# A graph layer and a mixture of experts on one core: gating and first-choice routing in batches beside the update, and an expert layer without its transposes

## The reference

```python
h = layernorm(x)
msg = silu(concat(h[ei], h[ej], d2) @ mW1 + mb1)
msg = silu(layer_norm(msg) @ mW2 + mb2)
agg = segment_sum(msg, ei)
x = x + h + silu(concat(h, agg) @ uW1 + ub1) @ uW2 + ub2
t = layernorm(x)                       # tokens of the experts
probs = softmax(t @ router_w.T)
rw, re = top_k(probs, 2); rw = rw / rw.sum(-1)
out = t
for e in range(8):
    y = gelu(t @ w1[e] + b1[e]) @ w2[e] + b2[e]
    out = out + combine[:, e] * y      # rw where e is one of the node's two, else 0
return x + out
```

## Time and profile before

| | |
|---|---|
| three runs, median (lowest to highest) | 2658.04 us (2655.57 to 2659.8) |
| the profiled execution | 2656.25 us, of which the span is 2654.4 us |
| PE / PEld busy | 2380.0 (90%) / 2044.3 (77%) |
| DVE / ACT / POOL busy | 2007.8 (76%) / 1716.5 (65%) / 1353.1 (51%) |
| TensorE's granted clock, mean | 0.949 of full |
| DMA | 265.16 MB, mean 100 GB/s |

### The profile page before, as it was taken

The page is one execution under the profiler, slowest core; times in us unless marked ns, Lnnn a source line. Parts: engine busy times, 40 slices in busy tenths (PEclk is TensorE's granted clock), DMA queues, the critical chain, the costliest instruction groups (busy, mean ns, idle before and its releaser), DMA issues. The chain is left out here.

```text
span 2654.4 us, 61287 instructions
## 1 busy us (share of the span) xinstructions
PE 2380.0 (90%) x15214; PEld 2044.3 (77%) x15215; DVE 2007.8 (76%) x6154; ACT 1716.5 (65%) x5986; POOL 1353.1 (51%) x1342
## 2 busy tenths in 40 slices
PE   4399999789999999999999999999999889119997
PEld 4288887568888888888888888888888779117886
DVE  8999999477777777777777777777777656546653
ACT  1777777567777777777777777777777556233432
POOL 2067777465555555555555555555555101267666
PEclk7599999989999999999999999999999989559998
DMA  7011111243232323232322332323235299156675
GB/s 151 1 34 29 34 34 29 86 114 91 87 92 87 91 87 91 87 91 87 91 87 89 89 91 87 91 87 91 87 91 86 62 289 307 67 204 203 208 123 65
DMA packets 155377, 265.16 MB, mean 100 GB/s; under 512 B 31249, under 2 KB 99440, under 8 KB 154917
## 3 DMA queue, kind: packets, MB, share of 16 engines
q0 software_dynamic: 64656, 147.39, 21.2%
q1 hardware_dynamic: 90623, 116.59, 14.6%
HBM read 190.85 MB, written 73.02 MB: 99 GB/s over the span
## 5 line engine op out<-in xcount | busy, mean ns | idle before, releaser
L1056 POOL DMA_INDIRECT work<-dst_half,stage_i x848 | 811.6, 957 | 758.3 <-PE ps L1264 582.5
L1247 PE MATMUL ps<-W2c,work 128*128 128x256 f32 x3392 | 802.3, 379 | 0.0
L1247 PEld LDWEIGHTS ps<-W2c,work 128*128 128x128 f32 x3392 | 612.0, 190 | 70.7
L1082 DVE TENSOR_TENSOR agg<-agg,ps 125x256 f32 x848 | 354.2, 418 | 254.0 <-PE ps L1264 246.3
L1188 ACT ACTIVATE work<-ps 128x512 f32<-128x512 f32 x424 | 251.9, 594 | 351.5 <-PE ps L1264 351.4
L1264 PE MATMUL ps<-work 128*125 128x256 f32 x1696 | 435.2, 379 | 1.3 <-ACT work L1209 1.3
L1203 ACT ACTIVATE work<-work 128x256 f32<-128x256 f32 x848 | 341.4, 404 | 53.6 <-DVE work L1109 50.1
L1161 DVE SCALAR_TENSOR_TENSOR work<-ps,work,b2c 128x256 f32<-128x256 f32 x848 | 368.4, 476 | 0.0
L1238 PE MATMUL ps<-ablk,work 128*128 x2544 | 351.1, 275 | 16.3 <-DVE work L1130 10.4
L519 POOL DMA_INDIRECT edge_records<-stage,work x208 | 262.6, 1263 | 176.2 <-PE ps L946 113.2
L1195 ACT ACTIVATE work<-work 128x256 f32<-128x256 f32 x848 | 340.8, 406 | 0.3
(11 more groups left out here) (280 smaller groups left out, 3366.8 us busy)
## 6 DMA issues: line engine op xcount, KB each, us to landing
work<-tile_sources SPq DMA_DIRECT2D x106, 250.0 KB
first_choice_tokens<-work SPq DMA_DIRECT2D x14, 1028.0 KB
work<-dst_half,stage_i POOLq DMA_INDIRECT x848, 2.8
second_choice_tokens<-work SPq DMA_DIRECT2D x14, 516.0 KB
work<-first_choice_tokens SPq DMA_DIRECT2D x28, 258.0 KB, 3.7
work<-second_choice_tokens SPq DMA_DIRECT2D x28, 258.0 KB, 2.9
work<-first_choice_tokens SPq DMA_DIRECT2D x28, 256.0 KB, 3.4
update_node_half<-work SPq DMA_DIRECT2D x25, 250.0 KB, 2.2
```

The source lines that it names most:

```text
L1056: pool.indirect_dma_start(bg[:, r, u, :], None, dstd, bass.IndirectOffsetOnAxis(ap=stage_i[:, c:c + 1], axis=0)).then_inc(gath[r], 16)
L1082: v.tensor_tensor(d, d, ps[0:NB, (7, 0)[a.mod(2)], u * D:(u + 1) * D], ALU.add).then_inc(agg_add, 1)
L1247: last = t_.matmul(ps[:, 5 + s, u * D:(u + 1) * D], sT[:, a.mod(RT), u, k], W2c[:, k], start=(k == 0), stop=(k == KC - 1))
```

## The change

It has three parts.

1. **Gating and routing in batches.** The 25 pairs of the update are split in batches of 9, 9 and 7 pairs. As soon as the logits of a batch exist, its gating chain runs in the four steps that follow, on the DVE behind that step's update work (`shift_logits`, `choose`, `count`, `place`). The pipeline has 36 steps instead of 31. The tiles of the first batch are routed two in a step (steps 19 to 27), those of the second three in a step (28 to 33), and the 14 of the last all in step 35. A table now can't be sorted by expert as a whole: each batch opens new tiles where its expert's last one is full, and `state` carries this from batch to batch. The table of experts is sent to memory and read back beside the last 14 tiles.
2. **Pads.** The harmless rows are kept in a table `pad_rows` in memory, which SP fills in the preparation, from `rec`. They are copied from there to the two tables in the message stage, two DMAs more in each of its 106 loads of one-hot rows, and three tiles of each table at the end of the preparation. The 28 stores of the update, and the wait for the tile they were made from, are gone. The waits for `zeros_out` now include the four stores to `pad_rows`.
3. **Experts.** The first matrix is multiplied with its weights as the stationary operand (eight products of 128 x 128 by 128 in place of four of 128 x 128 by 256 for a pair), so the result comes out transposed and L1988 and ACT's copy L1932 go. The bias is now one value for a partition, and ACT adds it with the Gelu (four of 128 x 128 for a pair). [...] The first bias on the DVE goes. The lags are shorter, and `y_ps` has four banks.

```diff
+BATCHES = (9, 9, 7)
+PACE = (2, 3, BK)
...
 # preparation, SP
+                empty = rec[:, :, :].rearrange("p g f -> p (g f)")[:, 0:2 * XB]
+                for h in range(XD // 2):
+                    sp.dma_start(padd[2 * h * P:2 * (h + 1) * P, :].rearrange("(p d) w -> p (d w)", p=P),
+                                 empty).then_inc(zeros_out, 16)
...
+                sp.wait_ge(pad_rows_out, 16)
+                for g in range(TAILS // 2, XC):
+                    d = g % XD * P
+                    for k in range(K2):
+                        sp.dma_start(xsd[k][g * P:(g + 1) * P, :], padd[d:d + P, 0:(XW if k else XB)]).then_inc(xpads_out, 16)
...
 # preparation, DVE
-                dve.wait_ge(zeros_out, 64)
+                dve.wait_ge(zeros_out, 64 + 8 * XD)
                 block_one_hots(NG - 1)
...
 # messages, SP, in each load of one-hot rows
+                        d = m.mod(2 * XD) * (P // 2)
+                        slots = bass.ds(m.of(P // 2), P // 2)
+                        for k in range(K2):
+                            sp.dma_start(xsd[k][slots, :], padd[d:d + P // 2, 0:(XW if k else XB)]).then_inc(xpads_out, 16)
...
 # update
+        def routed(m):
+
+            n = 0
+            for b, t0, t1, first in batches:
+                n = max(n, min(n + PACE[b] * max(m - first - 4, 0), t1))
+            return BK if m >= USTEPS else n
...
 # update, DVE (choose, count and place are the old chain cut to a batch, place with 5 wide and some 15 small operations)
+                for m in range(USTEPS):
+                    step(Step(0, 1, m))
+                    for b, t0, t1, first in batches:
+                        if m == first:
+                            shift_logits(b, t0, t1)
+                        if m == first + 1:
+                            choose(b, t0, t1)
+                        if m == first + 2:
+                            count(b, t0, t1)
+                        if m == first + 3:
+                            place(b, t0, t1)
+                    for t in range(routed(m), routed(m + 1)):
+                        r = t % RS0
+                        dve.wait_ge(slots_ready, batch_of(t) + 1)
+                        wait(dve, first_out[r], 16 * (t // RS0))
+                        v.tensor_scalar(ts0[n_, r, 0:D], agg[n_, t, :], mv3[n_, t:t + 1, 1], mv3[n_, t:t + 1, 0], ALU.mult, ALU.add)
+                        v.tensor_copy(ts0[n_, r, D:XW], idgate[n_, 0, t, :]).then_inc(row_ready, 1)
...
 # experts
-        LXT, L1, LG1, L2H, LHT, L2 = 1, 2, 3, 4, 5, 6
+        LXT, L1, LG1, L2 = 1, 2, 3, 4
...
 # experts, DVE, at the head of step m
+                    a = m - LXT
+                    if 0 <= a < XP:
+                        wait(dve, h_ps, a - RW + 1)
+                        for u in range(2):
+                            o = offs[2 * (b + L2 - LXT) + u]
+                            v.tensor_copy(w1p[:, a % RW, u], w1f[:, :, bass.ds(o, D)]).then_inc(w1p_ready, 1)
                     for i in beside(m):
                         route(i)
-                    a = m - L1
-                    if 0 <= a < XP:
-                        dve.wait_ge(h_ps, a + 1)
-                        wait(dve, hg_ready, a - 1)
-                        for u in range(2):
-                            o = offs[2 * (b + L2 - L1) + u]
-                            last = v.tensor_tensor(hb[:, a % 2, u], ps[:, 2 + a % 2, u * D:(u + 1) * D], b1b[:, bass.ds(o, D)], ALU.add)
-                        last.then_inc(hb_ready, 1)
...
 # experts, ACT
+                        for u in range(2):
+                            o = offs[2 * b + u]
+                            for f in range(KC):
+                                c = (u * KC + f) * P
+                                last = nc.scalar.activation(hT[:, a.mod(RH), c:c + P], ps[:, 2 + a.mod(2), c:c + P], ACT.Gelu,
+                                                            bias=b1b[:, bass.ds(o + f, 1)])
...
 # experts, PE
-                        wait(pe, hb_ready, a.of(1, -1))
+                        wait(pe, hT_ready, a.of(1, -1))
+                        pe.wait_ge(w1p_ready, a.of(2, 2))
                         for u in range(2):
-                            o = offs[2 * (b + L2 - L1) + u]
-                            for k in range(KC):
...
+                            for f in range(KC):
+                                for k in range(KC):
+                                    last = t_.matmul(ps[:, 2 + a.mod(2), (u * KC + f) * P:(u * KC + f + 1) * P],
+                                                     w1p[:, a.mod(RW), u, k, f * P:(f + 1) * P], xsT[:, a.mod(RH), (u * KC + k) * P:(u * KC + k + 1) * P],
+                                                     start=(k == 0), stop=(k == KC - 1))
...
-                        wait(pe, yb_ready, a.of(1, -1))
+                        wait(pe, yb_ready, a.of(1, 1 - RH))
...
-                    a = m - L2H
-                    if a.within(XP):
-                        pe.wait_ge(hg_ready, a.of(1, 1))
-                        wait(pe, hT_ready, a.of(1, -1))
-                        for u in range(2):
-                            for k in range(KC):
-                                c = (u * KC + k) * P
-                                last = t_.transpose(ps[:, 4 + a.mod(2), c:c + P], hg[:, a.mod(RH), u, k * P:(k + 1) * P], ident[:, :])
-                        last.then_inc(h_tr, 1)
```

More of the change, by code:

```diff
@@ L73 @@
 XD = 8
-assert XT + 16 <= P
+assert XT + 16 <= P and TAILS % 2 == 0
 class Step:
@@ L159, in gnn_moe_kernel @@
                nc.dram_tensor("second_choice_tokens", (XC * P + BK * (P - NB), XW), f32).ap()]
+        padd = nc.dram_tensor("pad_rows", (XD * P, XB), f32).ap()
         xtabd = nc.dram_tensor("tile_experts", (P, 1), i32).ap()
@@ L1295, in gnn_moe_kernel @@
         rwr = wcut(D)
+        b1r = wcut(D)
         ub1T = wcut(KC)
@@ new lines, in count @@
+                def count(b, t0, t1):
+                    c = slice(t0, t1)
+                    tk_, sl_ = by_expert(taken, t0, t1), by_expert(slot, t0, t1)
+                    for k, oh in ((0, oh1), (1, oh2)):
+                        link(v.tensor_copy(tk_[:, k * X:(k + 1) * X, :], oh[n_, c].rearrange("p t e -> p e t")))
+                    v.tensor_reduce(out=xcnt[n_], in_=tk_, axis=AX.X, op=ALU.add).then_inc(xcnt_ready, 1)
+                    n = XK * (t1 - t0)
+                    link(v.tensor_tensor_scan(slot[n_, 0:n], onex[n_, 0:n], taken[n_, 0:n], 0.0, ALU.mult, ALU.add))
+                    link(v.tensor_tensor(rsum[n_, c], m1[n_, c], m2[n_, c], ALU.add))
+                    link(v.tensor_scalar(rsum[n_, c], rsum[n_, c], 1e-12, None, ALU.max))
+                    link(v.reciprocal(rsum[n_, c], rsum[n_, c]))
+                    for k, top in ((0, m1), (1, m2)):
+                        link(v.tensor_tensor(idgate[n_, k, c, 1], top[n_, c], rsum[n_, c], ALU.mult))
+                    link(v.tensor_scalar(bscale[n_, c], mv3[n_, c, 1], 1.0, None, ALU.add))
@@ L1529, in step @@
                                              ACT.Copy).then_inc(tT_ready, 1)
-                update(act, step)
+                for m in range(USTEPS):
+                    step(Step(0, 1, m))
+                    for b, t0, t1, first in batches:
+                        if m == first + 1:
+                            act.wait_ge(sh_ready, b + 1)
+                            nc.scalar.activation(pr[n_, t0:t1], lg[n_, t0:t1], ACT.Exp).then_inc(ex_ready, 1)
+                    for t in range(routed(m), routed(m + 1)):
+                        r = t % RS0
+                        act.wait_ge(slots_ready, batch_of(t) + 1)
+                        wait(act, first_out[r], 16 * (t // RS0))
+                        nc.scalar.activation(ts0[n_, r, XW:XB], agg[n_, t, :], ACT.Identity, bias=mv3[n_, t:t + 1, 0],
+                                             scale=bscale[n_, t:t + 1]).then_inc(base_ready, 1)
             @block.tensor
@@ L1562, in step @@
                         last.then_inc(y2_ps, 1)
+                    for b, t0, t1, first in batches:
+                        if m.c == first + 3:
+                            pe.wait_ge(xcnt_ready, b + 1)
+                            t_.matmul(ps[:, 6, 0:XK], tri2[n_, :], xcnt[n_], start=True, stop=True).then_inc(xpre_ready, 1)
+                            t_.matmul(ps[:, 7, 0:XK], ones2[n_], xcnt[n_], start=True, stop=True).then_inc(xpre_ready, 1)
                     a = m - U1
```

426 lines of the change are left out of this document (219 added, 207 removed).

## The result

| | before | changed |
|---|---|---|
| median (lowest to highest) of 10 runs each | 2658.53 us (2655.57 to 2661.76) | 2650.24 us (2648.09 to 2654.64) |
| the profiled execution | 2656.25, span 2654.4 | 2649.79, span 2648.0 |

The ratio is 0.9971, with a 95% interval of 0.9963 to 0.9980: the changed kernel is 0.3% faster. The forecast was 2757 us with a range of 2702 to 2820, and it was wrong.

The account below looks back on a forecast made before the run. PE bounds update and experts, with DVE's chain and POOL's 50 scatters between; DVE bounds the preparation, PE the messages. Experts +119, update and routing -32, pads +11, copies +3, on 2656.25: 2757 us, range 2702 to 2820.

Parts of the forecast that it names:

- the loop: Experts: DVE weight copies and PE's two matrices wait on each other, 6.42 then 6.16 us a step; +119 us with additions.
- Two buffers for the copies don't help: Experts: a copy is delayed by its place in the DVE's order, so double buffering the copied weights gains nothing.
- the loop doesn't bind: Experts: rival in which PE's steps take 3.99 us and the kernel gets faster, 2621 us; chance 7%.
- The lock between DVE and POOL: Experts: DVE weight copies slowed by POOL's scatters through shared SBUF ports, 0.2 us a step added (0 to 1).
- The rival of 18%: Experts: the port lock holds for whole scatters, the second copy waits 0.96 us, 39 us more, 2796 us; chance 18%.
- The clock: Experts: PE's granted clock falls behind idle times of some 2.4 us, 0.35 us a step on average (0 to 1.3).
- Update and routing: Update to experts' start: dropped pad stores, batched gating and scatters beside the update, 227 instead of 259 us, -32 (-20 to -45).
- Pads: Preparation: DVE waits for the pad_rows stores, +11 us (7 to 14); six copies +3 (0 to 6); messages 0 (0 to +15).
- The tail: End of the kernel, behind PE, POOL issuing its last result: stays as it is, within 3 us.

Follow-up runs that it names:

- experiment 1: Changed kernel with the DVE copying the first-matrix weights for pair m-2 instead of m-1 in step m, so without slack: 2789.13 us, ratio 1.0498 to before.
- experiment 2: Changed kernel with LB = RX + 1 instead of RX + 2, so SP asks for base rows one step earlier: 2635.11 us, ratio 0.9919 to before.
- experiment 5: Changed kernel with the copies of first-matrix weights made by ACT instead of the DVE: 2647.49 us, ratio 0.9961 to before.
- experiment 7: Changed kernel, whose POOL idles 6.93 us within its last 14 scatters, with the table of experts stored only after the last routed row: 2648.80 us, ratio 0.9967.

## Why the prediction was wrong

- **The step that failed** is in the paragraph on the experts that closes the loop: "PE's first matrix for pair m, in step m+1, waits for the copy". It is in step m+2. The wait exists, its price was right to 0.1 us (6.34 and 6.07 measured in experiment 1 against 6.42 and 6.16), and the order had been read rightly except for that one constant. The sentence "Two buffers for the copies don't help" hangs on it and is wrong too: with a step between copy and use, the code needs two buffers to make the slack usable (no run has one buffer). The loop's 6.1 us have two steps of PE to fit in, 7.9 us, so in the second half PE's steps last 3.95 us and not 6.71, and the experts became 4 us longer and not 119. Experiment 1, which makes the kernel what that sentence said it was, gave 2789 us, within the forecast's range.
- **The forecast's own check could have caught it.** The rows of the order show waits by name, and not pairs. I set "m-1" beside L1967 and L2057 without counting in the trace. PE's first rows of the experts, in the kernel before, would have told:

```profile
2372.29 2.98 PE L1957 MATMUL ps<-ident,work 128*128 128x128 f32 x12 [83.99 <-DMA work<-first_choice_tokens]
2375.06 2.69 PE L1967 MATMUL ps<-ablk,work 128*128 x8
2377.58 0.60 PE L1957 MATMUL ps<-ident,work 128*128 128x128 f32 x4
```

  Twelve transposes, three pairs of them (0, 1, 2), stand ahead of the first L1967, that of pair 0. So the first matrix is two pairs behind the transposes.
- **The experts without the loop.** The rival "the loop doesn't bind" had 7% and gave 2621 us. Its outcome is the one that came true, and its PE step of 3.99 is 3.95. The condition that it was given is not: the DVE's work between PE's two matrices is as long as forecast, and the loop is open because it spans two steps. It was 29 us short. 9 of them are the update's (-22.7 for -32), the pads give back 2, and 21 are the experts' (+4.1 for -17). Of these 21, 16 are the base rows (286.2 us from the first transposes to the end, 270.4 in experiment 2), which no step of the forecast had: I had listed `LB` neither as moved nor as left. The rest stands in the first twenty steps. The rival had 93 us for them, 4 scatters of 1.27 us a step less some 8 us for the buffers. With the base rows early it is 101.2 us from the first transposes to the second bias of pair 15, so those 8 us were not there. In the changed kernel it is 104.0.
- **The lock between DVE and POOL.** I added 0.2 us a step, on the side of the copies. The trace shows it on POOL's side: 0.23 us for one of two results a pair in the second half, and 0.41 from 2480 to 2525 us (experiment 5). The two copies take 0.74 to 0.76 us in most steps, and 0.80 to 0.98 in ten of 56. The Trainium skill, SBUF — State Buffer, "SBUF: two separate sides", says that whoever starts first keeps the shared ports for its whole instruction and the other is blocked. On POOL's side the size agrees: 0.41 us is the length of one copy, and with the copies on ACT it goes. On the DVE's side it doesn't: the copies at 2400.21 start inside a scatter (2399.95 to 2401.08) and take 0.75 us as ever, and no copy is longer by a scatter's length. The rival of 18%, in which a copy waits for the rest of a scatter, has no room in experiment 1 either: its plain steps last 6.34 and 6.07 us, and two copies take 0.76.
- **The clock.** 0.35 us a step was given for idle times of about 2 us. In experiment 1, where these are real, 18 of 55 steps lost 1.6 us and 5 lost about 4 (1.2 of it the registers), 0.9 us a step. Too low, within the bounds given (0 to 1.3). In the changed kernel the granted clock is 0.97 from 2400 to 2500 us and 1.00 from there on.
- **Update and routing**: -22.7 against -32 (-20 to -45). By parts: 199.6 us from the first transposes to the last 14 tiles, and with the 5.5 us ahead of them 205 against 203. Then 24.4 for 14 scatters instead of 18, for the hole of experiment 7, and 7.1 to PE's start instead of 6.
- **Pads**: +8.7 for the zeros (7 to 14 given) and +3 for the six copies, and +0.5 in the messages, all as forecast, though the DVE's wait ended at 57.62 and not "near 60".
- **The tail**: "the end stays as it is, within 3 us": -3.1 us from the last pair to the end.

## What to carry to other kernels

A loop across two engines is priced in two numbers, its length and how many steps of the pipeline it spans. The length can be right to a tenth of a microsecond and the forecast still wrong by 4%, so count the span in pairs, on the rows of the trace, and never from the lags' names. And when a lag is shortened, list every constant that was set against it: a load that is asked for "n steps ahead" in another engine's order (here `LB`) keeps its own distance, and comes late without any instruction of its own having changed.

## What the runs showed of the hardware

- A DMA of 0.5 KB in 128 pieces of 4 bytes took 9.1 us to land beside scatters and 7.9 us beside the last two of them (2348.66 to 2356.55). The first of the four scatters beside it kept its buffer for 10.3 us (2330.30 to 2340.61), where in the kernel before 50 scatters followed each other every 1.27 us with four buffers.
- TensorE's granted clock stayed at 1.00 behind an idle time of 1.85 us in one step of experiment 1 and fell behind the same idle time in the next. By their lengths, 23 of the 55 steps have such a fall. What decides which steps do, the rows don't tell.
- A copy of 128x512 f32 on the DVE beside POOL's scatters lengthens the scatter's issue from 1.55 to 1.78 us where the scatter adds, and from 0.96 to 1.37 where it overwrites and starts under the copies. Two copies take 0.74 to 0.76 us in 46 of 56 steps, also where they start inside a scatter's issue.
